# Pass two of a two-layer metaformer kernel: where a chunk's turn and row copy stand, and which engines issue its table stores

## What is computed

```
# layer 0: mixer is a selective scan (pass one), then a feed-forward net
x = x + mixer0(ln_c(x))                      # scan, local conv, gate, out_proj
t = t + ffn(ln_t(t), W1, b1, W2, b2)         # fp8 products, 96 -> 384 -> 96
# layer 1: mixer is a modulated deformable convolution
v = ln_c(x)
offset, mask = conv3x3(v, offset_w), sigmoid(conv3x3(v, mask_w))
for k in range(9):                           # taps
    samp = bilinear(v, py + dy[k], px + dx[k]) * mask[k]
    out += einsum('bchw,oc->bohw', samp, weight[:, :, k])
x = x + out + bias
t = t + ffn(ln_t(t), W1, b1, W2, b2)
```

## Time and profile before

| what | value |
|---|---|
| median of 3 runs | 18195.23 us (18183.98 to 18203.86) |
| profiled execution | 18187.0 us, span 18185.2 us |
| busy over the span | VectorE 81%, TensorE 78%, GpSimd 65%, ScalarE 50% |
| mean granted TensorE clock | 0.805 |
| table stores | 1536 issues by SyncE, 72 KB each |
| gathers | 5184 issues by GpSimd, 4966 us busy |

### The profile page before, as it was taken

The page is one execution under the profiler, slowest core; times in us unless marked ns, Lnnn a source line. Parts: engine busy times, 40 slices in busy tenths (PEclk is TensorE's granted clock), DMA queues, the critical chain, the costliest instruction groups (busy, mean ns, idle before and its releaser), DMA issues. The chain is left out here.

```text
span 18185.2 us, 185966 instructions
## 1 busy us (share of the span) xinstructions
PE 14273.6 (78%) x51055; PEld 6830.3 (38%) x51055; DVE 14801.8 (81%) x19705; ACT 9045.4 (50%) x16414; POOL 11742.0 (65%) x9604
## 2 busy tenths in 40 slices
PE   7887877878778778778778765778787878787887
PEld 3333433333333333334333322333333333333333
DVE  5788788788788787887887874888888888888888
ACT  4555555555555555555555543444444444444443
POOL 3666666666666656666666663667676767776766
PEclk8988988888889889889888875767676766767666
DMA  2333333333333333333333334666666666666665
GB/s 60 88 95 89 87 92 93 87 93 90 90 89 91 91 91 88 94 89 87 93 93 86 91 86 129 175 175 181 175 180 175 181 175 183 175 184 176 180 173 153
DMA packets 1294664, 2229.07 MB, mean 123 GB/s; under 512 B 712841, under 2 KB 756125, under 8 KB 1281629
## 3 DMA queue, kind: packets, MB, share of 16 engines
q1 hardware_dynamic: 893022, 1086.35, 23.5%
q0 software_dynamic: 368640, 1076.24, 20.6%
q10 hardware_dynamic: 32256, 56.64, 1.0%
HBM read 1493.27 MB, written 271.92 MB: 97 GB/s over the span
## 5 line engine op out<-in xcount | busy, mean ns | idle before, releaser
L1271 POOL TENSOR_TENSOR hc<-h,crep 128x768 f32<-128x768 f32 x2304 | 4176.5, 1814 | 3631.5 <-DVE h L1071 2232.6
L1497 POOL DMA_INDIRECT G<-corners,idx x5184 | 4966.1, 958 | 2274.0 <-issue 1649.2
L710 PE MATMUL ps<-hc,sel 128*96 128x512 f32 (+1 forms) x9216 | 3919.8, 554 | 629.6 <-POOL hc L1271 483.3
L1055 DVE TENSOR_TENSOR ps<-dxr,ps 128x768 f32<-128x768 f32 x2304 | 2186.7, 949 | 1499.2 <-PE ps L699 1494.4
L1071 DVE TENSOR_TENSOR_SCAN h<-decay,carry,ps 128x768 f32<-128x768 f32 x1536 | 2776.8, 1808 | 208.5 <-ACT decay L893 148.6
L710 PEld LDWEIGHTS ps<-hc,sel 128*96 128x96 f32 x9216 | 1539.2, 182 | 2573.7 <-issue 1755.2
L893 ACT ACTIVATE decay<-dtr,a_neg 128x768 f32<-128x768 f32 x2304 | 2120.4, 926 | 263.1 <-DVE h L1071 243.0
L699 PE MATMUL ps<-bq,pick 96*128 96x512 bf16 (+1 forms) x4608 | 1275.2, 362 | 1212.8 <-DVE h L1071 905.0
L1786 DVE TENSOR_TENSOR G<-G,ps 128x1152 f32<-128x1152 f32 (+1 forms) x1152 | 1724.8, 1497 | 0.0
L790 PE MATMUL ps<-xcp,w_local 96*96 96x384 f32 x3456 | 1507.2, 559 | 3.2 <-ACT local_c L965 1.4
L1528 PE MATMUL ps<-cols_t,w_def 96*96 96x384 f32 x3456 | 1330.8, 546 | 177.4 <-ACT prow L1716 172.1
(11 more groups left out here) (218 smaller groups left out, 23341.6 us busy)
## 6 DMA issues: line engine op xcount, KB each, us to landing
crep<-c_rows SPq DMA_DIRECT2D x3072, 96.0 KB, 2.4
dtr<-rel SPq DMA_DIRECT2D x2304, 96.0 KB, 2.1
dxr<-mag SPq DMA_DIRECT2D x2304, 96.0 KB, 2.2
corners<-prow SPq DMA_DIRECT2D x1536, 72.0 KB
G<-corners,idx POOLq DMA_INDIRECT x5184
x_in<-in_x SPq DMA_DIRECT2D x32, 864.0 KB, 6.3
local_all<-local_c ACTq DMA_DIRECT2D x192, 144.0 KB, 2.4
sim<-sorted_rows SPq DMA_DIRECT2D x32, 864.0 KB, 6.0
```

The costliest lines, as they stand in the source:

```text
L710: m = pe.matmul(wide(BY, C)[:, a:b], Wt["sel"][:, cg, :], hc[:, v % HC, a:b], start=(v % ROUND == 0), stop=(v % ROUND == ROUND - 1))
L1055: dve.tensor_tensor(drive, dxr[:, q % 2, cg, :], drive, ALU.mult).then_inc(S["s_drive"], 1)
L1271: pool.tensor_tensor(hc[:, s % HC, :], h[:, s % HR, :], crep[:, g % CRING, :], ALU.mult).then_inc(S["s_weighted"], 1)
L1497: pool.indirect_dma_start(M["G"][:, slot(g), k, :], None, dram["tables"][side(r)], bass.IndirectOffsetOnAxis(M["idx"][side(r)][:, t, k:k + ...
```

## The change

In each period, at place 0: TensorE transposes xflat right behind the second layer of stream e and before the second part of the samples; ScalarE, behind y, waits for the turn, makes the row copy, waits for its own copy and issues four stores (corner row a = 1) under a semaphore of its own, p_astore. SyncE issues the other four (a = 0) before the output's store, and waits until they have landed before that store. GpSimd's wait at the first tile of an image, and the reuse of prow, wait for both semaphores. The diff, with the new function:

```diff
+    def store_corners(engine, d, a, done):
+        view = dram["tables"][side(d[0])].rearrange("(y x) (q c) -> y x q c", x=PW, c=C)
+        for b in range(2):
+            for r in range(2):
+                y0 = 8 * d[1] + r + 1 - a
+                dst = view[y0:y0 + 2 * ROWT - 1:2, 1 - b:1 - b + W, 2 * a + b, :]
+                engine.dma_start(dst.rearrange("t x c -> x t c"),
+                                 M["prow"][r * W:(r + 1) * W, d[1] % 2]).then_inc(done, 16)
...
@@ SyncE
+                if d is not None:
+                    sp.wait_ge(S["p_row"], nth(of_d, w) + 1)
+                    store_corners(sp, d, 0, S["p_store"])
+                    stored += 4 * 16
+                    sp.wait_ge(S["p_store"], stored)
                 if f is not None:
                     sp.wait_ge(S["p_y"], nth(of_f, w) + 1)
...
-                if d is not None:
-                    sp.wait_ge(S["p_row"], nth(of_d, w) + 1)
...
-                                sp.dma_start(dst.rearrange("t x c -> x t c"),
-                                             M["prow"][r * W:(r + 1) * W, d[1] % 2]).then_inc(S["p_store"], 16)
-                                stored += 16
-                    sp.wait_ge(S["p_store"], stored)
...
@@ GpSimd, first tile of an image
-                    pool.wait_ge(S["p_store"], 8 * 16 * nth(of_d, NCH * r))
+                    pool.wait_ge(S["p_store"], 4 * 16 * nth(of_d, NCH * r))
+                    pool.wait_ge(S["p_astore"], 4 * 16 * nth(of_d, NCH * r))
...
@@ TensorE: the transposes of xflat, unchanged in themselves
-                if u == 1 and d is not None:
+                if u == 0 and d is not None:
...
@@ ScalarE, behind y (L1706)
+                if u == 0 and d is not None:
+                    act.wait_ge(S["p_turn"], nd + 1)
+                    if nd:
+                        act.wait_ge(S["p_astore"], 4 * 16 * nd)
+                    if nd >= 2:
+                        act.wait_ge(S["p_store"], 4 * 16 * (nd - 1))
+                    act.activation(M["prow"][:, d[1] % 2], ps[0:PT, BN, 0:ROWT * C].rearrange("p (a b) -> p a b", b=C),
+                                   ACT.Copy).then_inc(S["p_row"], 1)
+                    act.wait_ge(S["p_row"], nd + 1)
+                    store_corners(act, d, 1, S["p_astore"])
...
-                if u == 2 and d is not None:
-                    act.wait_ge(S["p_turn"], nd + 1)
-                    if nd >= 2:
-                        act.wait_ge(S["p_store"], 8 * 16 * (nd - 1))
-                    act.activation(M["prow"][:, d[1] % 2], ps[0:PT, BN, 0:ROWT * C].rearrange("p (a b) -> p a b", b=C),
-                                   ACT.Copy).then_inc(S["p_row"], 1)
```

More of the change, by code:

```diff
@@ L364, in build_program @@
                      "p_xq1", "p_hid", "p_rnd", "p_bias", "p_quant", "p_lin1", "p_yr1", "p_yb1", "p_x2",
-                     "p_ctr2", "p_sq2", "p_var2", "p_rs2", "p_xn", "p_pad", "p_edge", "p_turn", "p_row", "p_store",
+                     "p_ctr2", "p_sq2", "p_var2", "p_rs2", "p_xn", "p_pad", "p_edge", "p_turn", "p_row", "p_store", "p_astore",
                      "p_off", "p_offs", "p_oturn", "p_osplit", "p_step", "p_index",
@@ L1481, in _ @@
                 sp.wait_ge(S["p_out"], 16 * outs)
+            if nth(of_d, PERIODS):
+                sp.wait_ge(S["p_astore"], 4 * 16 * nth(of_d, PERIODS))
             if next_before(PERIODS):
@@ L1597, in _ @@
                     m.then_inc(S["p_turn"], 1)
+                if u == 1 and c is not None:
+                    pe.wait_ge(S["p_mix"], nc_ + 1)
+                    if w % NCH == LASTP:
+                        pe.wait_ge(S["p_gate"], next_before(w) + 1)
+                    if d is not None:
+                        pe.wait_ge(S["p_xn"], nd + 1)
+                    pe.matmul(ps[0:C, BM, 0:CH], M["wg"][:], M["mix"][:, part(c[1])], start=True,
+                              stop=True).then_inc(S["p_proj"], 1)
                 if u == 3 and c is not None:
```

## The result

| kernel | median | runs | ratio to before (95%) |
|---|---|---|---|
| before, on the same chip | 18199.54 us | 18183.98 to 18206.38 | |
| after | 18373.70 us | 18371.33 to 18381.69 | 1.0098 [1.0080, 1.0115] |

The changed kernel is 174 us slower. The profiled execution has a span of 18369.9 us, 184.7 above that of before, and all of it is in pass two: its first xflat starts at 11024.5 us before and at 11020.0 after.

What follows compares the result with a forecast made beforehand. Convolve's start and length were taken to set ordinary periods, with no engine full. Ordinary periods +298, sixth periods +28 and block ends -16 gave +310 us, forecast 18500 us (from 18187.0, plus 8 for the median), range 18130 to 18600.

Steps and rivals of the forecast that it cites:

- The bound and the path: Pass two: no engine is full; convolve's start and length set an ordinary period, through VectorE's wait for rs ahead of xq.
- The rival with GpSimd's stall as the bound: GpSimd's wait for stores bounds the kernel: 264 us come back, 17930 us; chance 0.05.
- the one with two queues at once issuing more slowly: ScalarE's four issues take as long as eight now, 1.95 us more in all six periods: +363, 18860 us; chance 0.10.
- Steps 1 to 3: Transposes move early, adding nothing; row copy ends at 13722.2; four issues hold ScalarE 1.95 us, until 13724.2.
- The rival in which issuing costs ScalarE nothing: The four issues slip beside other work and convolve starts about 0.35 us earlier: 18135 us; chance 0.12.
- Step 4: Ordinary period: ScalarE's sample and xn copies follow the issues, so convolve starts 0.9 us later.
- Step 5: TensorE stands still 1.9 us ahead of convolve, its clock falls into convolve: 1.85 us on convolve, 1.5 on the period.
- The rival in which the clock holds: Only the later start of convolve is left: +124, 18315 us; chance 0.17.
- Second period: Second period of an image: 2.4 us of slack ahead of xq takes the 2.75 us nearly whole, cost 0.
- Sixth: Sixth period of an image: issues add 1.95 us to convolve's start, slack is 1.05, cost 0.9; 31 images, +28 us.
- Block ends: Eight block ends, where queues drain: the shorter GpSimd stall gives 2 us each, -16 us (bounds 0 and -68).
- The forecast's own range: The mechanism's range for the whole kernel, from 1.8 us to the full 2.75 a period: 18400 to 18600 us.

Runs made afterwards that it cites:

- e2: Turn and row copy at the places of the kernel before, stores split as in the change, ScalarE's four behind the row copy: 18146.60 us, 0.9968 of before.
- e3: Changed kernel, but ScalarE issues its four stores only behind its last sample copy; turn and row copy stay early: 18100.11 us, 0.9945 of before.
- e4: Changed kernel with two filler matmuls, whose results nobody reads, right before convolve: 18178.22 us, 0.9989 of before.
- e8: e3 with two filler matmuls, one before the second layer of stream e and one before convolve: 18042.72 us, 0.9911 of before.
- e6: e1 with four copies of a constant tile on ScalarE in the place of the issues: 18153.10 us, 0.9972 of before.
- e1: Changed kernel, but SyncE issues all eight stores ahead of the output's store and ScalarE none: 18108.64 us, 0.9949 of before.

## Why the prediction was right, and where its sizes were off

**The bound and the path.** Right. The stated range says little for it, since it holds both signs; the traces say more. GpSimd's stall for stores shrank by 120 us and the kernel got slower; what grew were the waits ahead of convolve and ahead of xq. The rival with GpSimd's stall as the bound, and the one with two queues at once issuing more slowly, are out: the median issue is 0.456 and 0.478 us, where it was 0.458.

**Steps 1 to 3.** Right. The rival in which issuing costs ScalarE nothing (18135 us) is out. The copy ends 2.3 us after the period's beginning (forecast 2.3), four issues take 2.1 us at the median (forecast 1.95), and ScalarE stands still for them. That the issuing costs ScalarE nothing is true only where nothing is due behind it: e2 and e3 have it at no cost. At an image boundary the four took 2.18 us, and the gather that waits for the landing started 6.63 us after their beginning (14052.83, shown below):

```profile
14046.20 2.18 ACTq L1416 DMA_DIRECT2D corners<-prow  x4
```

The Trainium skill ("DMA: Bandwidth & Descriptors", "Issuing engines are not separate DMA queues") calls the issue time usually small relative to the DMA; here it is about a third of the time to landing. That sentence doesn't speak of what stands behind the issues on their engine, and so didn't argue for the rival as the prediction has it: 0.478 us each on the chain to convolve cost 274 us over the kernel (changed kernel less e3).

**Step 4, the start of convolve: +0.9.** Right in place, a little large. Convolve starts 0.76 us later in the mean of the held periods (5.64 against 4.88), and these are 0.72 us longer: 123 x 0.72 = +88 us.

**Step 5, the clock: +1.5.** The mechanism was right in half of the periods and is measured there; that the price came out near is partly luck. The gap looked as the earlier trace rows had it: clock 1.00, TensorE busy 1.67 of 3.40 us, then 0.50, then 1.00 again before convolve ended. This happened in 60 of 123 ordinary periods, not in all. A period in which it did is 1.96 us longer than a held one (36.64 against 34.68), not 1.5. The 1.5 came from a pair whose slow member was no fall but a late rise, and one at the mild end of 17. The late rises themselves, for which the prediction has no term, went from 17 to 30 and from 2.84 to 3.18 us over a held period. By these numbers the clock costs 60 x 1.96 = +118 us by falls and 30 x 3.18 - 17 x 2.84 = +47 us by late rises, together 1.34 us a period. One factor was too large (every period falls), the other too small (1.5 us), and a term was missing; the errors nearly cancel. Why the late rises became more was not tried.

The Trainium skill ("TensorE: Matmul & The Clock Gate", "Part 1: The HAM clock gate") would have had the clock fall only after an idle stretch; this stretch was half busy and the clock fell, so the trace disagrees.

The rival in which the clock holds (18315 us, periods of 35 us) is out by the measured 36.41 us and by the falls seen in the trace. The experiment that removed the falls (e4, 18178) came out 137 us lower than that rival. It has none of the late rises either, and the start of convolve, the sixth period and the block ends were all mis-sized to the same side.

So the ordinary period cost 0.72 + 1.34 = 2.06 us, not 2.4: +253 us instead of +298.

**Second period: 0.** Right, 0.14 us. (Its rows give xq at 16.48 us, not 16.46, which changes nothing.) **Sixth: +0.9.** Wrong sign. Convolve starts 2.0 us later (9.53 against 7.52 in the mean), as step 4's 1.95 has it, but it is 0.5 us shorter (8.56 against 9.10), and xq is 0.33 us later, not 0.9. Then VectorE's idling ahead of its next xq falls from 1.26 to 0.40 us, so that the period is 0.57 us shorter: -13 us instead of +28. Why that second wait shrinks was not tried.

**Block ends: -16, measured -52.** This term was the most mis-sized one. I read the earlier trace rows as GpSimd ending with the others, and took 2 of 8.5 us. The next block's first xflat shows otherwise. Timeline of before, VectorE (the last gather there starts at 14010.16):

```profile
14009.10 0.66 DVE L1801 TENSOR_TENSOR G<-ps,G 128x480 f32<-128x480 f32 x1
14026.22 0.55 DVE L1849 TENSOR_TENSOR xflat<-ps,rs 96x384 f32<-96x384 f32 x1 [16.46 <-PEq L162]
```

and of the changed kernel, VectorE and then GpSimd:

```profile
14079.49 0.66 DVE L1811 TENSOR_TENSOR G<-ps,G 128x480 f32<-128x480 f32 x1
14090.41 0.55 DVE L1859 TENSOR_TENSOR xflat<-ps,rs 96x384 f32<-96x384 f32 x1 [10.27 <-PEq L162]
```

```profile
14052.83 0.94 POOL L1503 DMA_INDIRECT G<-corners,idx  x1 [7.91 <-DMA corners<-prow]
...
14074.41 0.94 POOL L1503 DMA_INDIRECT G<-corners,idx  x1 [0.30 <-issue]
```

From the last gather's start to the next xflat it is 16.06 us before and 16.00 after, though VectorE ends 1.4 us before GpSimd in the one and 4.8 us after it in the other. At the same place of e2 it is 15.99, and the mean over the eight block ends is 15.68 before and 15.75 after. The next block keeps its distance from GpSimd's last gather, so all that the gathers come earlier counts there; what GpSimd does in the 16 us was not tried. It was 6.6 us, not 8.5, since the first gather started 3.3 us after the indices were ready (14049.53 by the trace), not at once. In all 31 images GpSimd's wait for the stores shrank by only 3.9 us each (344 to 224 us), not 8.5.

**The sum** by measured terms: +253 + 4 - 13 - 52 = +192 us, against +298 + 0 + 28 - 16 = +310. Of the 118 us between them 45 lie in the ordinary period, 41 in the sixth, 36 at the block ends, and the second gives 4 back. The forecast's own range, too, was set wider than its terms: 1.8 to 2.75 us a period give 18430 to 18548 us, not 18400 to 18600.

**What the change consists of,** by the runs: the split and the earlier landing gain 48 us (e2), the earlier turn and copy 46 us more (e3), and the four issues ahead of the sample copies lose 274 us. How much of the 274 is the clock's has no single answer: e3 loses to 57 late rises what the changed kernel loses to falls and late rises. With the clock held in nearly every ordinary period on both sides (e4 against e8) the two places of the issues are 135 us apart.

## What to carry to other kernels

A DMA issue has a price on the engine that gives it, here 0.48 us; it is free where that engine has nothing due, and it costs more where TensorE behind it stands still until its clock falls (here in 60 periods behind gaps of 1.53 to 2.73 us, in none behind 0.94 us). Look at the clock when the long matmuls start: one that hasn't risen yet and one that falls while they run take different remedies. Price either with the share of periods that change and the mean of many such periods, not with one pair. At a loop's end look for the engine from whose last instruction the next block keeps a constant distance: a stall that nobody waits for inside the loop counts in full there.

## What was not expected of the hardware

- **Work for nobody made the kernel faster.** Two matmuls ahead of convolve took 196 us off the changed kernel (18373.70 to 18178.22), one at each of two places 57 us off e3 (18100.11 to 18042.72), with TensorE's mean granted clock at 0.826 and 0.820.
- **The mean clock didn't show the loss.** It was 0.805 before and 0.808 after, though the clock was low in convolve in 17 ordinary periods before and in 90 after. What counts is where in the period it is low.
- **A steep edge.** Convolve 0.6 us later (5.1 to 5.7 us after the period's beginning) goes with 221 us (e6 to the changed kernel), 0.6 us before that (4.5 to 5.1) with 44 us. No fall into convolve was seen at 5.1 us, and 60 at 5.7. The two ends differ also in what ScalarE does, so that the edge is read from two kernels and not from one size alone.
- **Starting earlier is half lost to the clock.** In e1 and e3 convolve starts 0.45 us earlier and the clock holds in 64 and 66 of 123 ordinary periods, against 106 before: held periods of 32.6 and 32.5 us beside others of 35.9 and 36.0, all of these with the clock still low when convolve starts.
- **The chip at 19476 to 19521 us for the kernel before,** with ScalarE idle for no shown reason, on two other chips.
